# Second feed-forward: where the down projection's products stand among the second attention's scores

## The reference

```python
# attention: 16 heads of 16 over all tokens of the block
scores = jnp.einsum('bhqd,bhkd->bhqk', q, k) / np.sqrt(HEAD_DIM)
attn = jax.nn.softmax(scores, axis=-1)
# feed-forward: 256 -> 1024 -> 256
D = jnp.dot(X.astype(jnp.float32), W0.T) + bias0
D = jax.nn.gelu(D, approximate=False).astype(jnp.float16)
E = jnp.dot(D.astype(jnp.float32), W1.T) + bias1
# and
x = x + s * _silu(E)
```

## Time and profile before

| | |
|---|---|
| Median of 3 runs | 917.71 us (917.7 to 919.16) |
| Profiled execution | 916.98 us, its span 915.2 us |
| Mean granted TensorE clock | 0.953 |
| TensorE busy | 796.7 us (87%) |
| VectorE busy | 619.5 us (68%) |
| ScalarE busy | 466.4 us (51%) |
| GpSimdE busy | 314.0 us (34%) |

### The profile page before, as it was taken

The page is one execution under the profiler, slowest core; times in us unless marked ns, Lnnn a source line. Parts: engine busy times, 40 slices in busy tenths (PEclk is TensorE's granted clock), DMA queues, the critical chain, the costliest instruction groups (busy, mean ns, idle before and its releaser), DMA issues.

```text
span 915.2 us, 13147 instructions
## 1 busy us (share of the span) xinstructions
PE 796.7 (87%) x4544; PEld 482.7 (53%) x4544; DVE 619.5 (68%) x1653; ACT 466.4 (51%) x948; POOL 314.0 (34%) x264
## 2 busy tenths in 40 slices
PE   3547496788999999998999999998999999988996
PEld 1324265574533666774533666774533666774533
DVE  3986757763985677673985677773985577763972
ACT  4556355323367667323367667222467576232464
POOL 0582856200200788200200788200201888200201
PEclk9877789998999999998999999998999999998999
DMA  7401001207400311008300311008200310017200
GB/s 240 124 21 41 18 1 47 76 0 213 88 1 13 93 54 30 2 12 222 68 2 17 90 53 30 1 22 227 53 2 19 87 30 1 1 33 213 56 3 24
DMA packets 54003, 53.27 MB, mean 58 GB/s; under 512 B 14513, under 2 KB 43569, under 8 KB 53937
## 3 DMA queue, kind: packets, MB, share of 16 engines
q1 hardware_dynamic: 50720, 47.60, 19.4%
q10 hardware_dynamic: 2896, 3.78, 1.4%
q0 software_dynamic: 320, 1.05, 0.4%
HBM read 39.00 MB, written 13.14 MB: 57 GB/s over the span
## 4 chain that ended last, share of the span: by engine, by line
PE 59%; DVE 12%; issue 9%; ACT 8%; POOL 7%; DMA 4%; ACTq 0%; SPq 0%; POOLq 0%; DVEq 0%
PE bank L883 9%; PE bank L988 6%; PE bank L1154 6%; PE bank L977 5%; PE bank L917 5%; PE bank L1142 5%; PE bank L1095 4%; PE bank L1049 3%; PE bank L1127 3%; DVE mx L1494 3%; POOL region L566 3%; DMA Kp<-scratch 2%; PE bank L927 2%; PE bank L1081 2%; PE bank L1132 2%
## 5 line engine op out<-in xcount | busy, mean ns | idle before, releaser
L1494 DVE TENSOR_REDUCE mx<-bank 128x1 f32<-128x512 f32 x256 | 162.1, 681 | 77.0 <-PE bank L1095 76.0
L566 POOL TENSOR_TENSOR region<-region 128x512 f32<-128x512 f32 x80 | 106.3, 1329 | 174.2 <-DVE region L1329 169.5
L883 PE MATMUL bank<-xnT,wrope 128*128 128x512 f32 x320 | 149.5, 609 | 18.4 <-ACT region L711 10.7
L823 ACT ACTIVATE region<-bank 128x512 f32<-128x512 f32 x256 | 136.3, 597 | 52.8 <-PE bank L1132 48.9
L728 ACT ACTIVATE region<-region,nb 128x128 f32<-128x128 f32 x256 | 81.6, 390 | 97.2 <-DVE nb L1336 97.1
L599 POOL TENSOR_TENSOR region<-region,bo_bc 128x256 f32<-128x256 f32 x16 | 11.7, 729 | 286.4 <-DVE region L1385 286.4
L883 PEld LDWEIGHTS bank<-xnT,wrope 128*128 128x128 f32 x320 | 59.1, 196 | 80.2 <-issue 71.3
L562 POOL TENSOR_TENSOR region<-region,sin_sb 128x512 f32<-128x512 f32 x60 | 80.5, 1342 | 24.4 <-ACT region L711 23.8
L1095 PE MATMUL bank<-Kp,Qp 64*128 64x512 f32 x256 | 74.2, 463 | 13.8 <-DMA Kp<-scratch 9.4
L917 PE MATMUL bank<-region 128*128 128x128 f32 x512 | 74.6, 291 | 11.3 <-ACT region L723 9.7
L1322 DVE TENSOR_TENSOR region<-bank,cos_sb 128x512 f32<-128x512 f32 x80 | 54.6, 688 | 42.5 <-PE bank L883 42.3
(11 more groups left out here) (135 smaller groups left out, 1338.3 us busy)
## 6 DMA issues: line engine op xcount, KB each, us to landing
wrope<-in_wrope SPq DMA_DIRECT2D x80, 128.0 KB, 2.1
scratch<-region SPq DMA_DIRECT2D x32, 256.0 KB, 4.2
Qp<-scratch SPq DMA_DIRECT2D x56, 128.0 KB, 4.0
Kp<-scratch SPq DMA_DIRECT2D x56, 128.0 KB, 4.4
X<-in_x SPq DMA_DIRECT2D x4, 512.0 KB, 4.0
scratch<-region SPq DMA_DIRECT2D x16, 128.0 KB, 3.9
out<-X SPq DMA_DIRECT2D x16, 128.0 KB, 2.1
VW<-v_rows SPq DMA_DIRECT2D x16, 102.0 KB, 2.8
```

The lines of the kernel that those rows point to most:

```text
L566: nc.gpsimd.tensor_tensor(dst, dst, tiles(sw[:, r % 2, :], i), ALU.add)\
L823: nc.scalar.activation(P1[:, n % 8, :], turned_bank(n)[:, :], ACT.Exp, scale=SCALE1)\
L883: mm = nc.tensor.matmul(misc(b, name)[:, 0:width], lhs(c), xnT[:, c, :], start=(c == 0), stop=(c == DC - 1))
L1494: nc.vector.tensor_reduce(mx1[:, g % 2, column:column + 1], s_ring[m % 3][:, :], AX.X, ALU.max)\
```

## The change

The first token tile of the down projection is placed ahead of the scores, right behind the up projection. Its products are ordered by chunk, and each chunk waits for its own GELU. The other three tiles follow six products per pair of scores, from the first pair on, so the last two of the 14 pairs have none. Tile t = 0 takes another bank, the others move along, and the first turned scores wait for one more bias add. The bias adds and gates on VectorE and the half tanhs on ScalarE get new places.

```diff
-UP_FIRST, DOWN_FROM, DOWN_STEP = 8, 3, 9
+DOWN_STEP = 6
...
-    jobs += [("dup", i) for i in range(HC)] + [("down", 0), ("down", 1), ("mt", 0), ("down", 2), ("down", 3)]
+    jobs += [("dup", i) for i in range(HC)] + [("down", 0), ("down", 1), ("down", 2), ("mt", 0), ("down", 3)]
...
-PLACED = {..., "down": (3, 4, 1, 2), "mt": (2,)}
+PLACED = {..., "down": (1, 3, 4, 1), "mt": (2,)}
...
                 half_tanh1(0)
+                half_tanh1(1)
                 max_high(0)
-                for t in range(1, TT - 1):
-                    half_tanh1(t)
+                half_tanh1(2)
...
-                            pe.wait_ge(e_ready.sem, e_ready.at(b, n + 1))
+                            pe.wait_ge(e_ready.sem, e_ready.at(b, n + 2))
...
-                def down(first, last):
-
-                    for m in range(first, min(last, TT * 3 * HC)):
-                        t, n = m // (3 * HC), m % (3 * HC)
-                        name = ("down", t)
-                        if n == 0:
-                            misc_take(pe, b, name)
-                        mm = nc.tensor.matmul(misc(b, name)[:, 0:DIM], H16[:, n % HC, t * P:(t + 1) * P],
-                                              w1T[:, n // HC, n % HC, :],
-                                              start=(n == 0), stop=(n == 3 * HC - 1))
-                        if n == 3 * HC - 1:
-                            misc_done(mm, name)
-
-                for i in range(UP_FIRST):
+                def down(t, first, last):
+
+                    name = ("down", t)
+                    if first == 0:
+                        misc_take(pe, b, name)
+                    for n in range(first, last):
+                        i, part = n // 3, n % 3
+                        if t == 0 and part == 0:
+                            pe.wait_ge(gelu_done.sem, gelu_done.at(b, i + 1))
+                        mm = nc.tensor.matmul(misc(b, name)[:, 0:DIM], H16[:, i, t * P:(t + 1) * P],
+                                              w1T[:, part, i, :], start=(n == 0), stop=(n == 3 * HC - 1))
+                    if last == 3 * HC:
+                        misc_done(mm, name)
+
+                for i in range(HC):
                     up1_job(i)
+                down(0, 0, 3 * HC)
                 for m in range(0, LEAD, 2):
                     if m == 4 * GH + 2:
                         turn_max(0)
                     scores_ahead(m)
-                    if UP_FIRST + m // 2 < HC:
-                        up1_job(UP_FIRST + m // 2)
-                    if m // 2 == DOWN_FROM:
-                        pe.wait_ge(gelu_done.sem, gelu_done.at(b, HC))
-                    n = DOWN_STEP * (m // 2 - DOWN_FROM)
-                    down(max(n, 0), n + DOWN_STEP)
+                    t, first = 1 + m // 2 * DOWN_STEP // (3 * HC), m // 2 * DOWN_STEP % (3 * HC)
+                    if t < TT:
+                        down(t, first, first + DOWN_STEP)
...
-                FFN_ROWS, GATES = (12, 17, 22, 27), (16, 21, 26, 35)
+                FFN_ROWS, GATES = (3, 12, 20, 28), (8, 17, 25, 35)
```

More of the change, by code:

```diff
@@ L83, in misc_order @@
     return order
-PLACED = {"xh": (0,), "qk": (1, 2, 3, 4), "v1": (5, 6), "dup": (1, 2, 3, 4), "down": (3, 4, 1, 2), "mt": (2,)}
+PLACED = {"xh": (0,), "qk": (1, 2, 3, 4), "v1": (5, 6), "dup": (1, 2, 3, 4), "down": (1, 3, 4, 1), "mt": (2,)}
 def misc_banks(order):
```

## The result

The change made the kernel no faster. The median is 921.67 us over 20 executions against 919.09 for the kernel before over 20: ratio 1.003, 95% interval 1.0016 to 1.0045. Measured again it was 922.15 against 919.12, ratio 1.0022 (1.0000 to 1.0043). The profiled execution took 919.0 us, span 917.2, mean granted clock 0.950. Every ratio here is to executions of the kernel before that were taken beside it; it comes from all of them except single ones that took far longer than the rest, so it is not exactly the quotient of two medians.

A forecast was written before the change was run, and what follows sets the result against it. The prediction took VectorE to bound the stretch from first maximum to second `turn_max`; 12.1 us saved over four sequences less 1.9 for later starts gave 10.2, so a median of 907.5 us, range 903.5 to 913.5.

The forecast's parts named there:

- What bounds: First maximum to second `turn_max`, 25.95 us, is a VectorE stretch; its waits for scores, 12.9 us in all, can be won.
- First tile: 24 down products, 2.9 us, fill TensorE's wait ahead of the scores; overruns lose 1.9 us over the sequences.
- Clock through the first pairs: TensorE no longer stops ahead of the scores, so full clock was expected through the first pairs.
- Six products behind each pair: A pair of scores takes 1.16 us on TensorE against VectorE's 1.20, so VectorE runs without a gap to the 28th maximum.
- VectorE's sum: VectorE's work from first maximum to second `turn_max` sums to 22.3 us, beside 25.95 before.
- SyncE's queue: Max rows land 1.4 us after last issue, before turning starts: cost 0; at the far end 2 us per sequence.
- the slack: Turning may start as late as about 18.2 us after the first maximum before VectorE notices.
- The wait at n = 2: Third turned-score matmul waits for the fourth bias add; TensorE stands about 1.5 us, costing 0.65 us per sequence.
- Everything behind 450.85 keeps its order and shifts.: From the second `turn_max` on, later head groups and the next front only move earlier by the gain.
- (a): Clock falls around the turned scores in one or two sequences, some 3.2 us each: 911 to 914; chance 0.20.
- (b): Clock falls behind the turned scores' start in all four sequences, 12.8 us back: 920.3, slower than before; chance 0.05.
- Sum: Savings of 2.8, 3.0, 3.3 and 3.0 us per sequence, together 12.1, less 1.9 for later starts: 10.2 us.

The follow-up runs named there:

- e4: Changed kernel with the fourth bias add after maximum 26 and group 0's max rows issued ahead of group 3's deal; 907.56 us, ratio 0.9862.
- e2_row26: Changed kernel with the fourth bias add after maximum 26 instead of 28; 916.69 us, ratio 0.9954 to the kernel before.
- e3: Changed kernel with group 0's max rows issued between the deals of groups 2 and 3 instead of behind both; 917.46 us, ratio 0.9971.
- e10: Changed kernel with the fourth bias add after maximum 26 and unused matmuls behind the last two pairs and ahead of turning; 909.9 us, ratio 0.9896.
- e6: Changed kernel with bias add at 26, max rows ahead of group 3's deal, and unused matmuls behind the last two pairs and ahead of turning; 906.06 us, 0.9865.
- e7: Changed kernel with bias add at 26, max rows ahead of group 3's deal, and nine products per pair, none behind the last six; 913.5 us, 0.9945.
- e1: Changed kernel plus 16 unused matmuls per sequence around the last two pairs and the start of turning, both stops left; 915.57 us, ratio 0.9944.
- e5: Kernel before plus unused matmuls: twelve ahead of the first scores, three behind each of the first three pairs; 911.52 us, ratio 0.9933.

## Why the prediction was wrong, point by point

*What bounds.* Right: the stretch from the first maximum to the second `turn_max` belonged to VectorE, and its idle time was what could be won. It fell to nothing up to maximum 27.

*First tile.* Right. 24 products took 2.7 us and hid the wait, but for 0.16 us in the fourth sequence. From the first up product the scores start at 13.07, 13.08, 13.07 and 13.30 us instead of 12.53, 13.54, 12.50 and 12.89: 1.1 us lost in all, where 1.9 was forecast.

*Clock through the first pairs.* Right, 1.00.

*Six products behind each pair, and VectorE's sum.* Right. VectorE has no gap up to the 28th maximum, and in e4, where the stops are gone, the second `turn_max` comes 22.3 to 22.5 us after the first maximum, where the sum had 22.3 without its charge for the stop. In the changed kernel it is 24.0 to 25.2 us, forecast 22.95.

*SyncE's queue.* Wrong. I gave landing 1.4 us after the last issue, from where the last packets were seen, and so a cost of nothing. In the changed kernel the deals end 14.5 us after the first maximum instead of 13.8, the four issues run 440.88 to 443.65, and the last begins near 443.0. Its last packets are over 1.4 us later, as in rows 10, but the packets' end was not the landing: turning starts at 445.15, 18.8 us after the first maximum, and the slack ended at 18.2. Below stand the issues of the last deal and of the four max rows, the deal's landing (4.1 us behind its issue), and two windows, the second inside the stop (the last columns are clock, DMA share, GB/s):

```profile
440.42 0.42 SPq L421 DMA_DIRECT2D Kp<-scratch  x1
440.88 2.77 SPq L463 DMA_DIRECT2D xnT_hi<-region  x4
```

```profile
Kp<-scratch SPq DMA_DIRECT2D x1, 128.0 KB, 4.1
```

```profile
440.00:443.00 3.00, 2.90 (x17) 1.66 (x15) 3.00 (x7) 0.42 (x1) 0.41 (x1) 1.00 1.03 216
444.50:445.10 0.60, 0.00 (x0) 0.00 (x0) 0.60 (x2) 0.00 (x0) 0.58 (x1) 1.00 0.00 0
```

The transfers of the deals fill the DMA engines up to 443, and the last lands at 444.5. In rows 10 no deal was under way. Over the four sequences turning starts 1.8, 2.1, 2.9 and 2.7 us after the last issue of the max rows was begun, but a steady 0.7, 0.6, 0.8 and 0.5 us after the last deal has landed; e2_row26 and the changed kernel profiled again have 1.8 to 3.0 and 0.6 to 0.9 us. So the max rows very likely come free only behind the deals ahead of them in the queue. No run tests that apart from the order of the queue, which e3 changes. The Trainium skill's 2.0 us ("DMA: Bandwidth & Descriptors", Anatomy of one DMA), which the page gives for transfers that GpSimdE issues, was nearer than my 1.4 for these that SyncE issues, but no fixed cost gives 1.8 to 3.0 us. By e10 against e6 this stop alone costs 2.9 us, 0.7 per sequence, at the edge of the noise. The edit that removes it (e3's) was cheap and lay in the queue's order that the step had walked through.

*The wait at n = 2.* The mechanism and about the size were right: n = 2 starts 20.8 after the first maximum (20.3 forecast), and 0.65 us per sequence was forecast against 0.7 after the fillers' overrun is taken off, which is an estimate.

*"Everything behind 450.85 keeps its order and shifts."* This is the step that failed. The order was kept; the durations were not, because the clock fell there. It stood in the text as rivals (a) and (b), with 0.20 for falls in one or two sequences and 0.05 for all four, and the sum had nothing for it. Rival (b) has the place and the four sequences right, but that its 920.3 lies so near the 921.7 measured is luck: it prices the falls at 4 x 3.2 = 12.8 us and the stops at 4 x 0.65 = 2.6, together 15.4; the runs show 7.9 for the clock and 7.3 for the stops, together 15.2. The price of a fall was too high: 6.8 us at half clock was to lose 3.2 over turned scores, and falls of 6.8 to 10.2 us lost about 2.0 per sequence. My reason against falls was that the work was denser than in the old thin stretch. The rows could not carry that: a stop of TensorE and single scores at VectorE's pace is what stood ahead of the old falls too, whose shortest wait was 1.98 us. I had also priced the two stops and the clock apart, although each stop lengthens the thin stretch: the falls last 30.7 us with both stops, 20.5 and 23.9 with one removed, and 3.4 with none. The Trainium skill's advice against long idle gaps ("TensorE: Matmul & The Clock Gate", HAM oscillation), read as I read it, that a stop of 1.5 us is harmless, does not hold here: falls follow stops of 1.1 us, and in e7 of 0.44.

*Sum.* Without both stops and nearly without falls the gain is 12.6 us (e4). The forecast's own figure without its charge for the stop at n = 2 is 10.2 + 2.6 = 12.8, so what it had up to the start of turning was right in size. The kernel with the stops and the falls has none of the gain.

## What to carry to other kernels

When matmuls are moved to fill a wait, look at the place they are taken from: if what is left there runs at another engine's pace, put a fall of the clock there into the sum, and give that case more than a small chance when the old place already showed falls. Here falls of 27 us in all cost 6.2 us in the old place and of 31 us cost 7.9 in the new one, so an edit that only moves them can eat its own gain. Before trusting such an edit, hold the clock with unused matmuls once: it splits clock from waits in one run, if the fillers end before the wait does. When a small transfer is moved up behind large ones, ask when the large ones land, and not only when the small one is issued.

## What the runs showed of the hardware that I had not expected

Sixteen unused 128x512 matmuls per sequence made the changed kernel 7.9 us faster (e1), and 21 made the kernel before 6.2 us faster (e5), both by the ratios. The clock fell in e7 with no stop of TensorE longer than 0.44 us in the 8 us ahead of it. Small copies of 4 KB let TensorE go 1.8 to 3.0 us after their last issue was begun, though their packets were over within 1.4 us of it; they had 128 KB transfers ahead of them in the queue, and TensorE went on 0.5 to 0.9 us after the last of those had landed (changed kernel twice, e2).
